# Conv with attention, then deformable conv: work ahead of the sampling loop reordered, folds to nine slots, the first far turn inside the loop, a shorter end

## What is computed

```python
# L0: two branches of 16 channels, each 3x3 conv + batch norm with given statistics
out = concat([fa * (map_a * scale1), fb * (map_b * scale2)])   # map: sigmoid of a 3x3 conv
                                                               # over (att, gh, gw, pr)
# L1: modulated deformable conv, 9 taps
offs = conv3x3(x, offset_w, offset_b)                # off_y, off_x for each tap
mask = 2.0 * sigmoid(conv3x3(x, mod_w, mod_b))
sy = off_y + hy + kyy;  sx = off_x + wx + kxx
sampled = bilinear_gather(x, sy, sx) * mask          # 0 outside the image
out = einsum('nckhw,ock->nohw', sampled, weight) + bias
out = relu((out - mean) * rsqrt(var + 1e-5) * gamma + beta)   # mean, var over n, h, w
```

## Time and profile before

| | us |
|---|---|
| median of 3 runs | 366.09 (365.16 to 371.99) |
| the run that was profiled | 368.4 |
| its span in the profile | 366.6 |

### The profile page before, as it was taken

One profiled execution on the slowest core, in us unless ns is written; L12 is line 12 of the kernel. 1 busy time (PEld: TensorE's weight loads), 2 busy tenths in 40 slices (PEclk: granted clock), 3 DMA queues, 4 the chain that ended last, 5 costly groups with the idle time before them and its releaser, 6 DMA issues.

```text
span 366.6 us, 16294 instructions
## 1 busy us (share of the span) xinstructions
PE 271.8 (74%) x7279; PEld 192.3 (52%) x7280; DVE 278.5 (76%) x507; ACT 239.0 (65%) x340; POOL 237.7 (65%) x182
## 2 busy tenths in 40 slices
PE   0479978699564779898988888888899887633540
PEld 0448413365142556576666666666666666523540
DVE  4851489818638879979999999999999999861376
ACT  1021474108438579779999999999999988722346
POOL 9000036917106279889999999999999999993000
PEclk9989999899965699989999999999999999995565
DMA  8880000000401300200000020000002000000006
GB/s 251 166 170 18 4 0 1 2 12 20 80 0 29 74 2 7 98 36 4 4 4 6 4 100 36 4 4 6 4 13 91 36 4 5 4 22 3 0 0 229
DMA packets 11749, 14.21 MB, mean 39 GB/s; under 512 B 4247, under 2 KB 7640, under 8 KB 11644
## 3 DMA queue, kind: packets, MB, share of 16 engines
q1 hardware_dynamic: 10218, 11.53, 10.9%
q10 hardware_dynamic: 1382, 1.04, 1.3%
q0 software_dynamic: 80, 0.61, 0.9%
HBM read 4.62 MB, written 2.98 MB: 21 GB/s over the span
## 4 chain that ended last, share of the span: by engine, by line
DVE 35%; POOL 29%; PE 18%; issue 6%; DMA 5%; ACT 4%; SPq 2%; POOLq 1%; DVEq 1%; ACTq 0%
POOL prod L505 17%; DVE prod L1241 17%; POOL prod L509 9%; PE ps L537 6%; DVE areg L1249 5%; PE ps L618 3%; DMA x_sb<-in_x 2%; DVE wreg L1145 2%; DVE x_sb L1325 2%; PE ps L548 1%; DMA hy<-xpad 1%; DVE prod L1107 1%; PE ps L723 1%; PE ps L636 1%; PE ps L798 1%
## 5 line engine op out<-in xcount | busy, mean ns | idle before, releaser
L723 PE MATMUL ps<-zreg,hx 64*64 64x96 f32 x4608 | 129.7, 253 | 25.6 <-DVE prod L1241 23.7
L1241 DVE TENSOR_TENSOR prod<-ps,hy 128x480 f32<-128x480 f32 (+1 forms) x256 | 138.0, 601 | 9.4 <-PE ps L723 3.4
L723 PEld LDWEIGHTS ps<-zreg,hx 64*64 64x64 f32 x4608 | 114.8, 136 | 45.7 <-ACT hx L955 30.1
L505 POOL TENSOR_TENSOR prod<-prod 128x832 f32<-128x832 f32 x64 | 125.8, 1965 | 15.5 <-DVE prod L1241 13.0
L878 ACT ACTIVATE hx<-ps 128x576 f32<-128x576 f32 x131 | 78.1, 648 | 34.9 <-PE ps L636 14.8
L955 ACT ACTIVATE hx<-hx,rbias 128x1152 f32<-128x1152 f32 x64 | 81.0, 1265 | 0.7
L509 POOL TENSOR_TENSOR prod<-prod 128x384 f32<-128x384 f32 x64 | 66.4, 1037 | 5.0
L1249 DVE TENSOR_REDUCE areg<-prod 128x64 f32<-128x512 f32 x64 | 44.5, 695 | 13.8 <-POOL prod L509 11.4
L636 PE MATMUL ps<-wz,xpad 32*64 32x144 f32 (+1 forms) x1024 | 35.2, 330 | 7.6 <-issue 4.0
L469 POOL TENSOR_TENSOR x_sb<-prod,x_sb 128x512 f32<-128x512 f32 x8 | 10.6, 1333 | 46.1 <-DVE prod L1107 46.1
L951 ACT ACTIVATE zreg<-ps 128x576 f32<-128x576 f32 x56 | 36.9, 659 | 0.0
(11 more groups left out here) (154 smaller groups left out, 285.7 us busy)
## 6 DMA issues: line engine op xcount, KB each, us to landing
zreg<-zreg SPq DMA_DIRECT2D x12, 288.0 KB, 2.3
out<-x_sb SPq DMA_DIRECT2D x8, 256.0 KB, 2.1
x_sb<-in_x SPq DMA_DIRECT2D x3, 512.0 KB, 4.8
preg<-scratch SPq DMA_DIRECT2D x16, 54.0 KB
zreg<-in_pos POOLq DMA_DIRECT2D x1, 528.0 KB, 5.7
x_sb<-in_x SPq DMA_DIRECT2D x2, 256.0 KB, 7.2
scratch<-prod SPq DMA_DIRECT2D x12, 36.0 KB
scratch<-zreg SPq DMA_DIRECT2D x12, 36.0 KB
```

The costliest lines, as they stand in the source:

```text
L505: pool.tensor_tensor(slots[:, :, 0:2 * moved], slots[:, :, 0:2 * moved], slots[:, :, 2 * KEPT:6 * KK], ALU.add).then_inc(half_folded, 1)
L723: return pe.matmul(g_ps(g, h)[u * W:(u + 1) * W, k - TAPS[h][0], :, :], hx[s, (t + u) % 4, k, :], z_sb[s, b, at:at + 3, k * C:(k + 1) * C] ...
L1241: mul = vector.tensor_tensor(pv[:, n0:n1], gv, wv[:, n0:n1], ALU.mult)
```

## The change

- **Map stage.** ACT writes the sigmoid in place in PSUM; DVE reads it from there. PE waits for `sig_used` instead of `sig_ready`. The clearing of `preg` goes; five small DMAs of constant rows stand in for it and for two. The matmuls of tile codes and `later` are made earlier.
- **Ahead of the loop.** The second norm has six pieces. PE makes lead rows 0 to 5 in banks 4 to 7 before and between the taps of conv 0, rows 6 and 7 within conv 1. ACT writes the high part of step 0 straight from PSUM (`save_high`), DVE makes the rest from PSUM (`split_bank`). Parts and rest of step 1 have buffers of their own (`parts1`, `rest1`); the wait at iteration 2 goes. ACT issues some of the stores and loads of step 0. DVE saves the offsets of step 1; two low splits, both `reaches` and the vertical weights of step 1 move into DVE's iterations 0 to 12, ACT's vertical distances of step 1 into its iterations 3 to 6.
- **Folds.** `SUMMED` goes from 8 to 9: the second fold has 320 elements, the reduce 9 slots. `REACH_TURN` goes from 8 to 15.
- **Far part.** The tables lie in `parts1`, cleared by one memset at iteration 9 and loaded behind the first ring close. The first turn of the first far tile is made within the last nine iterations: ACT stages two rows in each of iterations 55 to 60, PE multiplies one block in each of 57 to 62, ACT saves them in pairs, DVE prepares the weights at 61 and works out the codes of what is left at 62; sampling follows the last taps, product and reduction stand beside the last fold. `far_rows` starts behind that, with the copying shared by ACT and POOL.
- **End.** Eight banks; statistics from PSUM; one matmul for mean and second moment; norm and relu read PSUM but for the first chunk, which is cut in two.

The diff, cut to its core:

```diff
-SUMMED = 8
+SUMMED = 9
...
-        REACH_TURN = 8
+        REACH_TURN = 15
...
-        NORM2 = ((0, 17), (30, 49), (17, 30), (49, H))
+        NORM2 = ((0, 9), (30, 39), (9, 17), (39, 49), (17, 30), (49, H))
...
-                act.activation(sig[:, u, :], ps[:, (2 + u) * BANK:(3 + u) * BANK], ACT.Sigmoid)\
-                    .then_inc(sig_ready, 1)
+                act.activation(ps[:, (2 + u) * BANK:(3 + u) * BANK], ps[:, (2 + u) * BANK:(3 + u) * BANK],
+                               ACT.Sigmoid).then_inc(sig_ready, 1)
...
             pe.wait_ge(norm2, 2)
-            conv2_taps(0, range(KK)).then_inc(cv_ready, 1)
+            pe.wait_ge(wz_loaded, 16 * 4)
+            pe.wait_ge(later_ready, 1)
+            lead(0)
             pe.wait_ge(norm2, 4)
-            pe.wait_ge(later_ready, 1)
+            for n, t0, t1 in ((1, 0, 1), (2, 1, 3), (3, 3, 5), (4, 5, 7), (5, 7, 8)):
+                conv2_taps(0, range(t0, t1))
+                lead(n)
+            conv2_taps(0, range(8, KK)).then_inc(cv_ready, 1)
+            pe.wait_ge(norm2, 6)
+            pe.wait_ge(lead_low, 3)
+            pe.wait_ge(lead_saved, 3)
             conv2_taps(1, range(0, 3))
             turn_step(0)
...
+            def split_bank(b):
+
+                vector.wait_ge(high_ready, b + 1)
+                for u in range(2):
+                    half = slice(u * BANK // 2, (u + 1) * BANK // 2)
+                    ins = vector.scalar_tensor_tensor(
+                        rest[0][b][:, half].rearrange("p (r x) -> p r x", x=W),
+                        rows_of(ps[:, b * BANK:(b + 1) * BANK])[:, :, u, :], offbc[:, :],
+                        parts[0][:, 0, b, half].rearrange("p (r x) -> p r x", x=W), ALU.add, ALU.subtract)
+                ins.then_inc(rest_ready, 1)
...
-            split_step(0)
-            for n in DVE_LEADS[:2]:
+            for n in DVE_LEADS[:3]:
                 lead_row(n)
-            vertical_weights(0)
-            for n in DVE_LEADS[2:]:
-                lead_row(n)
-            split_step(1)
-            vertical_weights(1)
-            for s in range(STEPS):
-                reaches(s)
+            for b in range(B + 1):
+                if b < B:
+                    split_bank(b)
+                if b > 0:
+                    split_low(0, b - 1)
+            lead_row(DVE_LEADS[3])
+            for n in range(6):
+                vertical_weights(0, n)
+                if n >= 2 and n % 2 == 0:
+                    vertical_rest(0, n // 2 - 1)
+            vertical_rest(0, 2)
+            for b in range(2):
+                split_rest(1, b)
+            for b in range(B):
+                save_offsets(b)
+            for b in range(2):
+                split_low(1, b)
+                vector.wait_ge(parts_ready, B + b + 1)
+                split_rest(1, b + 2)
...
             for i in range(NT // 2):
                 weigh(i, 0)
                 weigh(i, 1)
+                if i < 2:
+                    split_low(1, i + 2)
+                elif i < 4:
+                    reaches(i - 2)
+                elif 4 <= i < 13:
+                    r, part_of = (i - 4) // 3, (i - 4) % 3
+                    if part_of < 2:
+                        vertical_weights(1, 2 * r + part_of)
+                    else:
+                        vertical_rest(1, r)
+                elif i == MAKERS + 5:
+                    first = first_far(vector)
+                    vector.wait_ge(first_tent, 1)
+                    mod = offs[:, ds(first[0], 1), ds(first[1] * NOFF + 2 * KK, KK)].rearrange("p a k -> p (a k)")
+                    chain(vector.scalar_tensor_tensor(far_w[:, :, :], far_u[:, :, :], -2.0,
+                                                      mod.unsqueeze(2).to_broadcast([P128, KK, 2]),
+                                                      ALU.mult, ALU.mult))
+                elif i == MAKERS + 6:
+                    begin = other_far(vector)
                 if i > 0:
                     add_up(i - 1)
...
+            vector.wait_ge(first_made, 1)
+            far_products(first_used)
             add_up(NT // 2 - 1)
+            vector.wait_ge(acc_ready, NT)
+            far_add(first[1], first[0])
...
-                if MAKERS < i <= MAKERS + B:
-                    pool.memset(z_sb[:, i - MAKERS - 1, 6:8, :], 0.0).then_inc(far_zeroed, 1)
+                if i == 9:
+                    pool.wait_ge(parts_stored, 16 * SPREAD * NPART * STEPS)
+                    pool.memset(far_tables, 0.0).then_inc(far_zeroed, 1)
...
-                if i == 2:
-
-                    act.wait_ge(px_ready[1], 16 * PX_DMAS)
...
+                m = i - MAKERS + 1
+                if m == 0:
+                    act.wait_ge(reach_ready, 2)
+                    first = first_far(act)
+                if 0 <= m < len(FAR_BLOCKS):
+                    stage_rows(act, far_row, copy, FAR_BLOCKS[m:m + 1], first[0], FAR_ROW).then_inc(first_staged, 1)
...
-                vector.wait_ge(outt_saved, c + 1)
-                vector.bn_stats(bstats[:, c, :], out_t[:, c * BANK:(c + 1) * BANK]).then_inc(st_ready, 1)
+                vector.wait_ge(outt_made, c + 1)
+                vector.bn_stats(bstats[:, c, :], ps[:, c * BANK:(c + 1) * BANK]).then_inc(st_ready, 1)
```

More of the change, by code:

```diff
@@ L365, in conv_deform_kernel, with stage_rows @@
         FAR = H + 2
         FAR1 = 128
[L367 to L371 removed]
+        FAR_LOADS = 16 * (B + 4)
+        FAR_ROW = 2
+        FAR_BLOCKS = tuple(itertools.product(range(2), range(3)))
+        FAR_LOW = ((0, 0), (0, 1))
+        FAR_HIGH = ((1, 0), (1, 1), (1, 2), (0, 2))
+        def stage_rows(eng, far_row, copy, pieces, y, row):
+            for i, ky in pieces:
+                for g in range(2):
+                    at = y * 2 + (g + ky - 1 + PAD_T) + (row * -1 if i else row)
+                    eng.reg_alu(far_row, at + FAR, FAR + PAD_T - 1, ALU.max)
+                    eng.reg_alu(far_row, far_row, FAR + PAD_T + H, ALU.min)
+                    eng.reg_alu(far_row, far_row, FAR, ALU.subtract)
+                    r = eng.snap(far_row, min_val=PAD_T - 1, max_val=PAD_T + H)
+                    ins = copy(far_x[:, i, ky, g * W:(g + 1) * W],
+                               xpad[:, ds(r, 1), 1:1 + W].rearrange("p a x -> p (a x)"))
+            return ins
@@ L372, in far_rows @@
+        def far_rows(eng, begin, tile, turn):
+            code, start = begin
+            tiles, turns = (eng.alloc_register(n) for n in ("far_tiles", "far_turn"))
             eng.reg_mov(tiles, 0)
             eng.reg_mov(turns, 0)
-            eng.reg_load(code, next_far[0:1, 0:1])
             with eng.While(lambda: eng.snap(code, min_val=0, max_val=NT * FAR1) < NT * FAR1):
@@ L930, in _ @@
+            for j in range(2, SPREAD):
+                store_part(act, 0, NPART - 1, j)
+            for n in range(4):
+                vertical(0, n)
+            act.wait_ge(parts_stored, 16 * SPREAD * NPART)
+            for j in range(SPREAD):
+                load_px(act, 0, j, 1)
+            save_lead(ACT_LEADS[3])
+            act.wait_ge(parts_ready, B)
+            act.wait_ge(cv_ready, 2)
+            for b in range(B):
+                save_conv2(1, b)
             for u in range(2):
```

512 lines of the change are left out of this document (296 added, 216 removed).

## The result

| | before | after |
|---|---|---|
| median of four runs, us | 368.36 | 338.3 (336.97 to 339.78) |
| profiled execution, its span | 366.6 | 338.0 |

One of the four runs before (371.99) was slow as a whole and is left out of the ratio, which is 0.921, with an interval of 0.911 to 0.932: faster by 8%. The forecast of 350.4, with a range down to 341, was too cautious by 12 us.

A forecast was written before the change was run, and what follows sets the result against it. The loop was held to be bound by two interleaved chains through POOL's folds, 3.11 us per iteration, with DVE only 0.06 below. Terms sum to -15.65 us, from the 366.09 median to 350.4; own range 346 to 354.5, overall 341 to 359.

The forecast's parts named there:

- part 4: Nine vertical operations moved into iterations 4 to 12: 4.1 themselves, 0.8 on ACT, 1.9 for a late operand; +6.8 us.
- the memset: One clearing of 1664 columns at iteration 9 delays a fold and a blocked vertical operation: +1.5 us.
- part 5: Folds to 9 slots: chain 6.16 for two iterations, but DVE alone becomes 3.12 and takes over the bound; +0.3 us.
- part 6: End of loop: four memsets gone -1.7, one at iteration 9 +1.5, ACT's staging +2.5, DVE's iterations 61 and 62 +3.0 us.
- Parts 1 to 3: Everything up to iteration 4's first weighing, which starts at 124.3 in place of 137.29: -13.0 us.
- part 1: Map stage: DVE reads the sigmoid from PSUM beside POOL; five periods fall from 1.92 to about 1.4, -2.6 us.
- part 3: Less work stands just ahead of the loop: first weighing at 109.3, iteration 4 at 124.3; -13.0 us including part 1.
- Parts 7 and 8: First far turn leaves the stretch after the last fold, -12.8 us; transposes, statistics and norm behind it shorten, -2.25 us.
- A: Rival: the work added in the loop hides, about -23 us in all, 343 us; chance 0.25.
- B: Rival: the earlier start is not had, gaining 7 in place of 13, about 356.5 us; chance 0.22.
- D: Rival: the first far turn does not leave the tail, some 12 us stay there, 362 us; chance 0.04.
- C: Rival: POOL takes the port, so DVE operations in the loop wait for folds, +19.5 us, 370 us; chance 0.07.

The follow-up runs named there:

- a_sig: Kernel after with the sigmoid written to SBUF again, so DVE's product has two SBUF inputs; 340.96 us (0.938).
- a_ahead: Kernel after with all vertical work of the second step done ahead of the loop; 340.03 us (0.931).
- a_ctrl: Kernel after, unchanged, measured again as a control; 337.78 us (0.923).
- a_light: Kernel after with both of POOL's folds cut to one slot each, sums left incomplete; 329.54 us, one run.
- b_sum9: Kernel before with folds to 9 slots and nothing else; 361.27 us (0.986).
- b_light: Kernel before with both of POOL's folds cut to one slot each, sums left incomplete; 353.42 us, one run.
- a_nofirst: Kernel after without the first far turn in the loop, the tail running the whole far turn; 346.47 us (0.940).
- a_staging: Kernel after with four extra 128x5 copies on ACT ahead of each of the six staged blocks; 340.50 us (0.933).
- a_late: Kernel after with the nine vertical operations of iterations 4 to 12 behind the add-up instead of ahead of it; 348.13 us (0.953).
- a_warm: Kernel after with six useless fp32 matmuls keeping PE busy between the last sample and the transposes; 337.33 us (0.922).

## Why the prediction was wrong, point by point

The forecast missed 13 us of gain: 7.5 in part 4 with the memset, 2.4 in part 5 and 6.1 in the rest of part 6, against 2.9 in the start, which gave less than forecast. Two kinds of step failed. The first is the bound: DVE was held to be within 0.06 of the loop's pace, so that nine slots could gain nothing and nothing put on DVE could hide. DVE alone needs 2.85 of 3.11, and the loop went to 3.02. The second, and by size the larger, are prices for waits and work that did not show in the loop at all: the late operand (1.9), ACT's vertical distances (0.8), its staging (2.5), and DVE's work in iterations 61 and 62 (3.0), with 1.0 too much for the memset.

**Parts 1 to 3, the start: -10.1 for -13.0, the direction right, most of it untested.** Only the buffer of part 1 has a run of its own (a_sig, 1.8 us) and the vertical work of part 3 (a_ahead, some 1.5 us); what the order of leads, the split and the buffers of step 1 give is seen in their sum alone. The first weighing starts at 113.06, where I had 109.3. Of these 3.8 us, 2.06 lie ahead of the map stage's chunk 2 and are for the most part the execution's own (a_ctrl), and 0.8 is part 1's (a_sig). These two already explain why the distances start at 104.81 and not at 102. The loads ahead of them landed 6.0 us after the last issue, and not the 3.86 of the earlier trace rows, but this issue (98.74) came as much earlier as they took longer. PE's timeline shows the wait for them:

```profile
104.81 0.66 PE L681 MATMUL ps<-preg,sel 26*128 26x288 bf16 x4 [4.00 <-DMA preg<-scratch]
```

The remaining 0.9 lies behind them: from the distances to the first weighing it took 8.25 us, and not 7.3. From the first weighing to that of iteration 4 it then took 14.1 us, and not 15.0, which gives the 0.9 back.

**Part 4 and the memset: +0.8 for +8.3.** The failed step is that DVE had no room, so that nothing hides an operation. DVE alone takes 2.92 + 0.48 = 3.40 (a_light), against iterations of 3.11 before: 0.3 for each of the nine, 2.6 and not 4.1. No operand came late, so the +1.9 for iteration 4 did not come, and ACT's four operations did not show either (+0.8; iterations 4 to 6 take 3.37 to 3.41). The memset cost 0.5, in iteration 10, and not 1.5. And two terms were missing. The far codes cost 1.4 in place of 2.8; most of the difference is the single iteration of 4.20 in the trace before, with the clock at 0.73. In b_sum9 the codes stand where they stood before and cost 1.5, so their move is not what saved it; whether the nine slots did or the execution is open. The seven iterations without a vertical operation or codes have part 5's gain, 0.6 together. (2.6 + 0.5 - 1.4 - 0.6 = 1.1, against the 0.8 measured.)

**Part 5: -2.1 for +0.3, the central error in kind, not in size.** "DVE alone becomes 3.12" rested on a timeline in which DVE seemed to wait for nobody. b_light, a_light and b_sum9 show 2.85, 2.92 and a loop of 3.02 bound by the pair of POOL's folds and DVE. The chain of part 5 itself, 6.16 for two iterations, was nearly right (6.04 to 6.05), and would have given the gain, had I not overruled it with DVE's false bound. The difference of 0.12 is the second fold's step, 0.24 and not 0.13.

**Part 6, the end of the loop: -2.3 for +3.8.** All three added terms came to next to nothing; a_nofirst has 0.07 for all of them together. ACT's copies take 0.40 per iteration and not 0.7 to 0.9, and with distances and weights make 2.85 of 3.02 (3.02 of 3.11 in the fullest iteration, 298.71 to 301.82). On DVE the operation of iteration 61, priced at 2.0 behind a fold, came ahead of it:

```profile
307.70 0.17 DVE L1442 SCALAR_TENSOR_TENSOR far_w<-far_u,offs 128x18 f32<-128x18 f32 x1
307.96 0.78 DVE L1421 TENSOR_REDUCE areg<-prod 128x64 f32<-128x576 f32 x1
...
307.86 1.96 POOL L573 TENSOR_TENSOR prod<-prod 128x832 f32<-128x832 f32 x1
```

DVE comes first here and POOL second, as in iteration 4; the earlier trace rows already had this order, and part 6 did not count on it. The register loads, priced at 1.0 in iteration 62, do not show: it takes 2.94. That they were done while the weighings ran is what this suggests; no row shows it. The memsets' -1.7 and eight periods shorter by 0.09 make -2.4, which is what was measured.

**Parts 7 and 8: -12.7 for -12.8 and -2.1 for -2.25.** Both right: 1.39 us remain behind the last add-up (I had 1.3), and the transposes run at half clock for their first 3 us (granted clock 0.50 from 319.04 to 322). From their start to the end of the statistics it took 6.61 in place of 7.79, which is 1.2 less, where I had 1.0. That part 8 came out to 0.2 is in part luck: its stretch of 18.96 is one trace's, and in a_ctrl it is 19.20, in a_staging 19.95. But the count of part 7 does not say what the turn's place in the loop is worth: that is 8.4 us (a_nofirst).

**Rivals.** A was nearest, and even it stopped at 343: it too had DVE within 0.06 of the period. B and D did not come. C came in a_late, and in the kernel after only in two operations, with some 0.5 each. The chances for faster came from the right cases; the range was too narrow on the fast side, as every added operation had been given a price and only one case let them off together.

## What to carry to other kernels

Before an engine is called the bound, add up its own instructions: a period in which it shows no idle time may still hold waits of 0.1 to 0.2 us, and in this kernel the sign was whether the reduce started 0.08 ahead of the weighings' end or 0.1 behind it. A gap that is still there when the other engine has next to no work, as the 0.10 ahead of each weighing, is no such wait. Cutting the other engine's work to almost nothing shows the pace directly, in one run. Where two engines exclude each other on a memory, put the small operation where its engine holds the turn already, ahead of the work that releases the other; the same nine operations cost 9 us more by their place alone. And price an addition by the cover on its engine: three terms of mine, 7.4 us together (1.9, 2.5 and 3.0), did not show in the loop at all, one because its operand wasn't late, one because ACT had room for it, and one because DVE came first and its register loads took nothing that shows.

## What the hardware showed that I had not expected

- POOL's two-tensor addition in fp32 is not linear in its length: 0.77 us for 256 elements per partition, 0.79 for 320, 1.04 for 384, 1.97 for 832.
- An operation of DVE with two SBUF inputs that comes first stretches POOL's fold to 2.21, by 0.24 only, though it overlaps it for about 0.4; one that comes second waits for the whole of what is left of the fold (1.86 for an operation of 0.57).
- Four copies of 128x5 on ACT in sequence with two of 128x64 take it from 0.39 to 0.77: about 0.1 each.
- PE's granted clock was at 0.50 for the first 3 us of the transposes after 5.9 us without matmuls (a_ctrl), and at 1.00 for all of them after a pause of 0.56 us (a_warm).
